# A gated decay scan with routed low-rank experts: the third group's router tasks one scan sooner, and unit 15's late half first on GpSimd

## The reference, cut to what matters

```python
# x, f: (4, 1024, 1024); per batch a decay per channel
ek, euk = exp(min(k, 30)), exp(min(u + k, 30));  ekv = ek * v
nf, df = forward scans of (ekv, ek):  a = a * decay + input
nb, db = the same scans backward in time
y = sigmoid(x) * (nf + nb - ekv + euk * v) / max(df + db - ek + euk, 1e-8) * (0.8 + 0.2 * tf)
h = silu(y @ rw1.T + rb1);  logits = (h @ rw2.T + rb2)[:, :16] + gates
coeff = softmax of the two largest logits, zero elsewhere          # 16 experts
base = y @ W.T + bias;  xa = y @ A          # rank 16 each, 256 columns
out = x + base + (xa * coeff spread over the ranks) @ B
```

## Time and profile before

| what | value |
|---|---|
| median of 3 runs | 682.92 us (681.83 to 688.22) |
| the profiled execution | 682.46 us, span 680.4 us |
| PE busy | 591.8 us, 87% of the span |
| DVE, ACT, POOL busy | 520.8, 360.2, 367.8 us (77, 53, 54%) |
| mean granted TensorE clock | 0.957 |

### The profile page before, as it was taken

How to read it: one execution, slowest core, us unless ns; L and a number is a source line. 1 busy time by engine, 2 the same in 40 slices (tenths; PEclk the granted TensorE clock), 3 DMA queues, 4 the chain that set the end, 5 groups by cost and what they waited for, 6 DMA issues and landing times.

```text
span 680.4 us, 6882 instructions
## 1 busy us (share of the span) xinstructions
PE 591.8 (87%) x2546; PEld 477.2 (70%) x2546; DVE 520.8 (77%) x579; ACT 360.2 (53%) x428; POOL 367.8 (54%) x183
## 2 busy tenths in 40 slices
PE   0153688879999936999999999999999999999997
PEld 0132576658878824788888887888788888888786
DVE  7999899998989999999879996999699322021202
ACT  6777899854765668457735574567454221011100
POOL 1789998866878777557535854485456401000100
PEclk9966799989999967999999999999999999999999
DMA  5324477525664832135413442326222402040122
GB/s 193 123 91 153 143 232 206 180 94 109 167 158 90 207 105 93 47 113 174 162 47 108 147 164 77 109 105 204 77 78 78 154 1 72 21 153 2 28 65 78
DMA packets 33249, 78.45 MB, mean 115 GB/s; under 512 B 4736, under 2 KB 4928, under 8 KB 33216
## 3 DMA queue, kind: packets, MB, share of 16 engines
q1 hardware_dynamic: 30912, 73.82, 33.2%
q0 software_dynamic: 2304, 4.20, 4.3%
HBM read 57.03 MB, written 20.97 MB: 115 GB/s over the span
## 4 chain that ended last, share of the span: by engine, by line
PE 65%; DVE 16%; POOL 6%; ACT 6%; issue 4%; DMA 3%; SPq 0%; POOLq 0%; ACTq 0%; DVEq 0%
PE acc L915 21%; PE acc L917 20%; PE acc L916 20%; DVE mix L726 3%; DVE mix L721 2%; DVE mix L747 2%; DVE mix L717 2%; DMA out<-xo 2%; DVE eu L736 2%; PE acc L926 1%; PE acc L927 1%; DVE yr L753 1%; DMA xo<-w_router_a 1%; PE acc L964 1%; POOL y_lo L624 1%
## 5 line engine op out<-in xcount | busy, mean ns | idle before, releaser
L915 PE MATMUL acc<-y_hi,wa_hi 128*128 128x512 f32 x640 | 259.2, 405 | 57.5 <-POOL y_lo L624 50.8
L916 PE MATMUL acc<-y_lo,wa_hi 128*128 128x512 f32 x640 | 255.0, 398 | 0.0
L917 PE MATMUL acc<-y_hi,wa_lo 128*128 128x512 f32 x640 | 254.6, 398 | 0.0
L915 PEld LDWEIGHTS acc<-y_hi,wa_hi 128*128 128x128 f32 x640 | 123.7, 193 | 90.4 <-POOL y_lo L624 52.2
L917 PEld LDWEIGHTS acc<-y_hi,wa_lo 128*128 128x128 f32 x640 | 123.5, 193 | 26.8
L916 PEld LDWEIGHTS acc<-y_lo,wa_hi 128*128 128x128 f32 x640 | 123.8, 193 | 24.9
L614 POOL TENSOR_TENSOR mix<-mix,kv 128x1024 f32<-128x1024 f32 x31 | 74.3, 2396 | 93.8 <-DVE mix L705 78.7
L760 DVE SCALAR_TENSOR_TENSOR xo<-acc,bias_sb,xo 128x512 f32<-128x512 f32 x64 | 46.7, 737 | 75.9 <-PE acc L917 75.7
L624 POOL TENSOR_TENSOR y_lo<-yr,y_hi 128x1024 fp32r<-128x1024 f32 x31 | 76.4, 2466 | 35.0 <-ACT y_hi L401 34.7
L637 POOL TENSOR_TENSOR wx_lo<-xa,wx_hi 128x512 fp32r<-128x512 f32 x16 | 20.8, 1318 | 118.4 <-ACT wx_hi L478 118.4
L726 DVE TENSOR_TENSOR_SCAN mix<-d_ps,mix 128x1023 f32<-128x1023 f32 x32 | 74.7, 2334 | 3.6 <-ACT mix L413 3.6
(11 more groups left out here) (105 smaller groups left out, 696.8 us busy)
## 6 DMA issues: line engine op xcount, KB each, us to landing
kv<-f_cm SPq DMA_DIRECT2D x32, 512.0 KB, 3.5
yr<-x_cm SPq DMA_DIRECT2D x32, 512.0 KB, 3.5
out<-xo SPq DMA_DIRECT2D x64, 256.0 KB, 3.3
xo<-x_cm SPq DMA_DIRECT2D x64, 256.0 KB, 3.7
out<-xo POOLq DMA_DIRECT2D x16, 256.0 KB, 6.0
xa<-w_base SPq DMA_DIRECT2D x5, 512.0 KB, 3.6
xo<-w_base SPq DMA_DIRECT2D x3, 512.0 KB, 6.1
xo<-w_router_a SPq DMA_DIRECT2D x2, 480.0 KB, 3.8
```

Of the source, the lines that this page charges most:

```text
L915: nc.tensor.matmul(out_ap, wh, yh, start=start, stop=False)
L916: nc.tensor.matmul(out_ap, wh, yl, start=False, stop=False)
L917: return nc.tensor.matmul(out_ap, wl, yh, start=False, stop=stop)
```

## The change

For group 2 alone the router tasks move from step 17 into step 16. On VectorE hidden stands right behind backward_den(16), silu behind sum_den(16), routing behind scale_e(17), and weigh behind ratio(16). ScalarE's tasks move to match: low_rows, copy_xa and sigmoid_z come right behind exp_k(17), and exp_gap, copy_turned and split_wx follow in steps 16 and 17. TensorE puts base(2, 1, 0 to 3) ahead of the logits, base(2, 2, 0 to 2) ahead of turn and base(2, 2, 3 to 4) ahead of spread. GpSimd takes gate_late(15) ahead of sum_n(15) and split_late_lo(15) ahead of gate_n(15), and split_wx(2) ahead of split_lo(16). No instruction is added or removed.

```diff
 # ScalarE, step s
-                if q == 1:
+                if q == 1 and G != SPLIT:
                     sigmoid_z(G)
...
+                if q == 1 and G == SPLIT:
+                    split_wx(G)
+                if third:
+                    scale_end_num(s)
+                    exp_k(s + 1)
+                    low_rows(G)
+                    copy_xa(G)
+                    sigmoid_z(G)
...
+                if third:
+                    exp_gap(G)
...
+                if third:
+                    copy_turned(G)
 # GpSimd
                 if s - 1 in HALVED:
                     sum_late(s - 1)
+                    gate_late(s - 1)
                 if 0 < s <= UNITS:
                     sum_n(s - 1)
                 if s - 1 in HALVED:
-                    gate_late(s - 1)
+                    split_late_lo(s - 1)
                 if 0 < s <= UNITS:
                     gate_n(s - 1)
                 if s - 1 in HALVED:
-                    split_late_lo(s - 1)
                     split_lo(s - 1)
+                if q == 1 and G == SPLIT:
+                    split_wx(G)
 # VectorE
+                third = s == first_step(SPLIT)
+                if q == 1 and G == SPLIT:
+                    weigh(G)
...
                 first_groups(s, AFTER_BWD_DEN)
+                if third:
+                    hidden(G)
...
                 first_groups(s, AFTER_SUM)
+                if third:
+                    silu(G)
                 if s + 1 < UNITS:
                     scale_e(s + 1)
-                if q == 0:
+                if third:
+                    routing(G)
+                if q == 0 and not third:
                     hidden(G)
 # TensorE
+                ahead = 4 if G == SPLIT else 0
+                if ahead:
+                    bank_in(G, 4)
+                    for kc in range(ahead):
+                        base(G, 1, kc)
                 if G != 1:
                     logits(G)
...
+                if G == SPLIT:
+                    pe.wait_ge(xa_copied, 2 * G + 1)
+                    for kc in range(3):
+                        base(G, 2, kc)
                 turn(G)
                 pe.wait_ge(xa_copied, 2 * G + 2)
                 if G:
-                    for kc in range(k0, k0 + 3):
+                    for kc in range(3 if G == SPLIT else k0, 5 if G == SPLIT else k0 + 3):
                         base(G, 2, kc)
                 spread(G)
```

More of the change, by code:

```diff
@@ L518, in _ @@
                     split_hi(s - 1)
-                if s < UNITS and q != 1 and not late_sigmoid:
+                if q == 1 and G == SPLIT:
[6 more added lines that the diff above has]
+                    sigmoid_z(G)
+                if s < UNITS and (q != 1 or G == SPLIT) and not late_sigmoid:
                     sigmoid_r(s)
@@ L528, in _ @@
                     split_hi(s - 1)
-                if q == 1:
+                if q == 1 and G != SPLIT:
                     copy_turned(G)
-                if s < UNITS and q != 1 and not late_sigmoid:
+                if s < UNITS and (q != 1 or G == SPLIT) and not late_sigmoid:
                     exps()
-                if s < UNITS:
+                if third:
+                    exp_gap(G)
+                if s < UNITS and not third:
                     scale_end_num(s)
-                if s + 1 < UNITS:
+                if s + 1 < UNITS and not third:
                     exp_k(s + 1)
@@ L548, in _ @@
                     exps()
-                if q == 0:
+                if q == 0 and G != SPLIT:
                     low_rows(G)
@@ L1056, in _ @@
                 bank_in(G, 4)
-                for kc in range(k0, CB):
+                for kc in range(max(k0, ahead), CB):
                     base(G, 1, kc)
@@ L1071, in _ @@
                 if G:
-                    for kc in range(k0 + 3, CB):
+                    for kc in range(5 if G == SPLIT else k0 + 3, CB):
                         base(G, 2, kc)
```

## The result

| what | before | after |
|---|---|---|
| median of 12 runs each | 684.6 us (681.63 to 688.22) | 687.1 us (684.78 to 691.22) |
| ratio after to before | | 1.0047 [1.0028, 1.0066] |
| profiled execution, its span | 682.46 us, 680.4 us | 688.79 us, 687.0 us |

With more runs the kernel before has a median of 684.6 us, not the 682.92 us of the first three. The change costs 0.47%: 3.2 us, 1.9 to 4.5 us by the interval. This is within 1%, so the same, slower side.

A forecast was written before the change was run, and what follows sets the result against it. TensorE's and VectorE's chains were taken to meet at block 7, with VectorE's the later: 3.5 + 0.6 - 1.75 = +2.35 us on the profiled 682.46 us, 684.8 us, or 685.3 us as a median; range 682.0 to 688.6 us.

The forecast's parts named there:

- The forecast: Whole kernel: +2.35 us on the profiled 682.46 us, 685.3 us as a median, counted as the same; chance 0.48.
- VectorE's chain: From backward_den(16) to evacuate(2, 2): idle 3.5 us at hidden and 0.6 at the logits, less 1.75 before, +2.35 us.
- What bounds the kernel: At block 7, about 297 us, TensorE's and VectorE's chains arrive together; a gain needs both sooner, a delay only one.
- TensorE's chain: Unit 15 to the logits: taken up 1.2 us sooner, the 2.43 us wait for the hidden layer gone, -3.6 us alone.
- the keys' transfer: Unit 17's keys ahead of exp_k(17): landing 3.3 us after their issue, with bounds of 3.2 to 3.8 us.
- Its cause: hidden's 3.5 us idle: low_rows queued behind exp_k(17), keys issued 1.23 us later by GpSimd's reorder, the old cover gone.
- The two together: TensorE at the experts and block 5: waits of 2.0 us for wx_lo and 3.8 us for evacuate(2, 0).
- The clock: Rival: TensorE's clock falls after the gap at block 5, costing 1.6 us more, 686.9 us; chance 0.28.
- the rival of a gain: VectorE isn't late, hidden starts below 262.35 us, TensorE's gain stays: 681.2 us, or 679.3 without the wx_lo wait; chance 0.18.
- A low clock up to the logits: Rival: lower clock through unit 15 and 12 base matmuls, logits at 271.9 us, +8.0 us, 690.9 us; chance 0.03.

The follow-up runs named there:

- k5: The kernel before with the three evacuations of step 18 about one scan sooner on VectorE; 684.82 us, ratio to before 1.0003.
- k9: The kernel before with the TensorE part of the change alone; 682.41 us, ratio to before 0.9967.
- k11: The kernel before with the TensorE part of the change and the three evacuations about one scan sooner; 681.46 us, ratio to before 0.9945.
- k4: The changed kernel with the three evacuations of step 18 about one scan sooner on VectorE; 681.66 us, ratio to before 0.9967.
- k1: The changed kernel with GpSimd's order on unit 15 as before; 687.95 us, ratio to before 1.0048.
- k3: The changed kernel with a second copy of unit 17's keys, issued when sum_n(15) has ended; 686.53 us, ratio to before 1.0031.
- k6: The changed kernel with unit 17's keys sent early and 12 base matmuls behind spread instead of ahead of the logits; 684.48 us, ratio to before 1.0009.
- k10: The kernel before with the changed GpSimd order on unit 15 alone; 687.3 us, ratio to before 1.0041.
- k7: The kernel of k6 with the three evacuations about one scan sooner as well; 680.13 us, ratio to before 0.9937.
- k12: The kernel of k7 with GpSimd's order on unit 15 as before; 681.43 us, ratio to before 0.9942.
- k8: The kernel before with the TensorE part and GpSimd's order on unit 15, no router task moved; 685.9 us, ratio to before 1.0039.
- k2: The changed kernel with 12 base matmuls taken from ahead of the logits and 12 others put behind spread; 688.04 us, ratio to before 1.0053.

## Why the prediction was right, and where it was off

The forecast was +2.35 us and the same; the measurement gives +3.2 us [1.9, 4.5], and as medians 684.6 and 687.1, inside the range. That the size fits as well as it does is partly luck. In the profiled executions VectorE's chain gives +3.37 us and the clock 2.32 more. The medians differ by only 2.5 us because one profile lies under its median and the other above; and the 685.3 us was counted from a median of three, 1.7 us under that of twelve.

- *What bounds the kernel.* Right: two chains meet at block 7. k5 and k9 show it from the two sides: early evacuations alone are worth nothing, and with the TensorE part alone TensorE waits for them (1.03 us). k11 has both and has a lower median than either (681.46 us against 684.82 and 682.41), though its interval overlaps that of k9.
- *TensorE's chain.* Unit 15 was to be taken up 1.2 us sooner: 1.05. It was to ask for the hidden layer at 267.9 us, 269.1 with the 1.17 us added: it asked at 268.6. It then still waited 1.60 us where I had nearly none, because the layer was late.
- *VectorE's chain*, the step that carried the forecast: right in its mechanism, off in one term. hidden's idle time was to be 3.5 us and was 4.63. The term that was mis-sized is the keys' transfer: I took the median of 3.3 us, with bounds of 3.2 to 3.8, and it took 4.4. In k4, with the same order on these engines, it took 3.8 us and hidden idled 4.03. The logits' 0.6 us was 0.49, and weigh had no idle time, as said. Sum: +3.37 us for +2.35.
- *Its cause.* Here the prediction told half. It put the whole 3.5 us on the keys and the cover that was removed. k1, k3 and k6 show a second hold of nearly the same size (in k3 2.8 of 3.7 us came back), TensorE's way to the logits, so removing the first brings little. Also, it has the reorder act through the keys' issue alone, and didn't name split_hi(15) on ScalarE, which waits 2.59 us for gate_n(15). In after that wait is over at 260.34 us, before the keys land, and costs nothing. In k10, in the old order of tasks, it makes scale_e(17) 1.4 us late and helps to lengthen TensorE's gap; with the keys early, VectorE idles 1.07 us ahead of hidden with it (k7) and 0.20 us without it (k12).
- *The two together.* wx_lo: 2.0 us said, 1.60 measured. Block 5: 3.8 us said, 3.64 measured.
- *The clock.* I gave this rival 0.28 and set it beside the forecast. In the profiled execution it came true: behind the 3.64 us gap 0.50 for 4.9 us, and it cost 2.32 us where I had 1.6. The Trainium skill, page "TensorE: Matmul & The Clock Gate", section "Why this matters for your kernels", says that an idle window between bursts puts the gate back to its lower clock. The trace agrees at this gap; how the lengths of gaps and the clock go together in the other traces stands in the last section. The median of after, 687.1 us, lies nearer to this rival's 686.9 than to 685.3, but the medians' difference of 2.5 us lies nearer to the forecast's 2.35 than to this rival's 3.95. How many executions of either kernel have such a stretch stays open, since one profile shows one execution.
- *The other rivals.* VectorE was late, so the rival of a gain fell: hidden started at 266.47 us, 265.30 without the offset, and the limit was 262.35. A low clock up to the logits didn't come either: the matmuls behind 259.13 were at full rate again from 263.5 us on.

## What to carry to other kernels

Before a task is moved ahead on in-order engines, list on each of them what it will stand behind and what covered it until now: here one copy, queued behind a transfer, lost its cover of 2.33 us, and VectorE idled 4.63 us for logits that came no sooner. When an edit removes a wait and the time stays, look for a second hold in the next row that idles before giving the theory up, and price the parts of a change in a two by two table, since two parts that hurt the same wait don't add up. Where a late engine frees the banks, the place of the freeing instructions can be worth more than the task that made it late: three evacuations moved up turned 687.1 into 681.66 us.

## What the runs showed of the hardware

- Gaps on TensorE and the granted clock behind them. After 1.03 us (k9) and twice 1.60 us (after) it stayed at 1.00. After 1.24 us (k7) it fell all the same, 2.4 us behind the gap's end: 0.51 over 3.5 us. After 2.83 us (k6), 3.04 us (k8), 3.46 us (k2), 3.61 us (k3) and 3.62 us (k1) the windows behind had 0.62 to 0.67 of it, over 4.0 to 5.1 us; after 3.64 us (after) and 3.70 us (k5), 0.50 over 4.9 us, and after 5.67 us (k10), 0.53 over 5.6 us. The length of the gap alone doesn't tell it: in before, 2.43 us and 2.58 us were followed by windows at 1.00 (269 to 275 us and 115.3 to 120 us; the earlier trace rows show the gaps). In the earlier trace rows a drop followed a window in which TensorE had 1.00 us of work in 3.3, and there was one behind 2.63 us in k2 (0.56 for 3.0 us).
- The transfer of one unit's keys, always the same bytes, landed 3.1 to 5.5 us after its issue over the 14 traces, near unit 17 (windows of 240 to 300 us). For unit 17 it was 4.4 us in after, 3.8 in k4, 3.7 in k2 and 3.3 in k1; the 5.5 us was one of k11. My bound of 3.8 us, the largest of four in one trace, was too small.
